# Two 64-wide attentions: reciprocal of the sums in four pieces between the maxima, product and more adds on GpSimd

## The reference, cut to what matters

```
# first layer, cross attention ("c"): 8 heads, queries from x (1024 a batch), keys and values from ctx (154 a batch)
sim = jnp.einsum('bihd,bjhd->bhij', q, k) * D ** -0.5
attn = jax.nn.softmax(sim, axis=-1)
out = jnp.einsum('bhij,bjhd->bihd', attn, v).reshape(B, Nq, H * D)

# first layer, feed-forward part ("m"): routed, 4 of 16 heads chosen for each batch, 1024 queries and 1024 keys
score = jax.nn.softmax(jnp.einsum('bhqd,bhkd->bhqk', Qs, Ks) * scale, axis=-1)
O = jnp.einsum('bhqk,bhkd->bhqd', score, Vs)
```

## Time and profile before

| | |
|---|---|
| median of 3 runs | 3031.12 us (3030.83 to 3033.93) |
| the profiled execution's own time | 3020.05 us |
| its span | 3018.5 us |
| busy of the span: TensorE / VectorE / ScalarE / GpSimd | 70% / 57% / 32% / 30% |
| mean granted TensorE clock over the span | 0.817 of 2.4 GHz |
| c: first maxima matmul to last product | 592.8 to 770.4 us |
| m: first exp to last product | 933.6 to 1133.9 us |

### The profile page before, as it was taken

One profiled execution on the slowest core, in us unless ns is written; L12 is line 12 of the kernel. 1 busy time (PEld: TensorE's weight loads), 2 busy tenths in 40 slices (PEclk: granted clock), 3 DMA queues, 4 the chain that ended last, 5 costly groups with the idle time before them and its releaser, 6 DMA issues. The chain is left out here.

```text
span 3018.5 us, 37236 instructions
## 1 busy us (share of the span) xinstructions
PE 2120.8 (70%) x13401; PEld 1081.7 (36%) x13405; DVE 1727.6 (57%) x3122; ACT 976.5 (32%) x1721; POOL 893.1 (30%) x1051
## 2 busy tenths in 40 slices
PE   3478888778557996299999981454485595529992
PEld 2224344322432224123333241232142253427992
DVE  2656664566537874277777515897774704436442
ACT  0246665133102331157777710111020020134330
POOL 0222221211022340457555311232263201052224
PEclk8779999878778997689999965555797797559996
DMA  4321110000010000501110032000110000053113
GB/s 133 157 59 37 43 43 7 18 1 0 10 25 1 1 1 16 198 12 32 33 32 25 9 99 66 1 2 3 42 56 28 14 30 4 24 183 126 50 50 94
DMA packets 86525, 133.20 MB, mean 44 GB/s; under 512 B 18309, under 2 KB 58257, under 8 KB 85329
## 3 DMA queue, kind: packets, MB, share of 16 engines
q1 hardware_dynamic: 76673, 118.70, 12.3%
q0 software_dynamic: 3664, 9.32, 1.0%
q10 hardware_dynamic: 6016, 2.89, 0.4%
HBM read 84.94 MB, written 45.68 MB: 43 GB/s over the span
## 5 line engine op out<-in xcount | busy, mean ns | idle before, releaser
L769 DVE TENSOR_REDUCE a_mneg<-a_SM 128x1 f32<-128x1024 f32 (+7 forms) x512 | 489.7, 986 | 232.4 <-PE a_SM L631 122.3
L752 ACT ACTIVATE a_P<-a_ST 128x512 f32<-128x512 f32 (+2 forms) x896 | 474.0, 556 | 243.1 <-PE a_ST L662 234.9
L631 PE MATMUL a_SM<-a_K,a_Q 96*128 96x512 bf16 (+2 forms) x896 | 271.8, 375 | 119.7 <-POOL a_V L583 109.0
L662 PE MATMUL a_ST<-a_Q,a_K 98*128 98x512 bf16 (+2 forms) x896 | 302.7, 368 | 17.3 <-ACT a_P L752 12.7
L680 PE MATMUL a_OP<-a_P,a_V 128*32 128x512 f32 (+3 forms) x1792 | 226.6, 567 | 5.2 <-ACT a_OT L732 3.5
L662 PEld LDWEIGHTS a_ST<-a_Q,a_K 98*128 98x128 bf16 x896 | 82.4, 103 | 242.6 <-ACT a_P L752 214.6
L631 PEld LDWEIGHTS a_SM<-a_K,a_Q 96*128 96x128 bf16 x896 | 85.7, 100 | 199.7 <-POOL a_V L583 109.7
L599 POOL TENSOR_SCALAR_AFFINE_SELECT a_P<-a_P 128x128 f32<-128x128 f32 (+1 forms) x256 | 77.1, 305 | 254.9 <-ACT a_P L752 252.9
L2775 DVE TENSOR_TENSOR experts_hl<-work 128x512 bf16<-128x512 f32 x92 | 83.8, 969 | 88.8 <-POOL work L2625 88.8
L2625 POOL CAST work<-work 128x512 bf16<-128x512 f32 x92 | 73.5, 838 | 198.9 <-PE experts_py L2709 183.7
L161 PE MATMUL n_turned<-ident,work 128*128 128x128 f32 x192 | 34.6, 365 | 133.5 <-DVE work L204 133.5
(11 more groups left out here) (504 smaller groups left out, 4475.2 us busy)
## 6 DMA issues: line engine op xcount, KB each, us to landing
work<-L_ffn_W SPq DMA_DIRECT2D x16, 1024.0 KB, 6.2
a_Q<-q_stacks SPq DMA_DIRECT2D x32, 384.0 KB, 3.8
a_K<-k_stacks SPq DMA_DIRECT2D x32, 384.0 KB, 4.7
conv_tab<-dft_tables SPq DMA_DIRECT2D x8, 1024.0 KB, 4.8
bias_hankel<-bias_rows SPq DMA_DIRECT2D x16, 448.0 KB, 3.4
k_stacks<-a_qkv_k_hi SPq DMA_DIRECT2D x12, 512.0 KB
q_stacks<-a_qkv_q_hi SPq DMA_DIRECT2D x12, 512.0 KB
expert_rows<-zeros SPq DMA_DIRECT2D x1, 5888.0 KB, 24.4
```

The costliest lines, as they stand in the source:

```text
L631: last = pe.matmul(SM[:, c % 2, k0:k0 + kn], Qs[0:KR, g % slots, u, qt * P:(qt + 1) * P], Ks[0:KR, g % slots, u, k0:k0 + kn], start=True, ...
L662: last = pe.matmul(out[:, c0:N], Ks[0:KX, g % slots, u, k * P:(k + 1) * P], Qs[0:KX, g % slots, u, qh * N + c0:(qh + 1) * N], start=True, ...
L752: act.activation(Pr[:, s % 2, u, j, c0:N], ST[:, (4 * s + x) % 2, c0:N], ACT.Exp, scale=scale).then_inc(exp_done, 1)
L769: dve.tensor_reduce(mneg[:, g % 2, u, qt:qt + 1], SM[:, c % 2, 0:width(qt)], AX.X, ALU.max, negate=True).then_inc(mx_read, 1)
```

## The change

The reciprocal of a unit's sums is made as four instructions of 128 columns each, `inverse(n, lo, hi)`, at hand-picked places of VectorE's loop; `den_read` now counts four a unit. The first number of a key of `pieces_at` is the step k, the second says whether the place is before (0) or after (1) the second maxima call; the value is how many units back, and the pieces. The product moves from VectorE to GpSimd, ahead of its add in a later step (`product_at`: step, units back). In m (`shared` True) each engine keeps its add, in c GpSimd makes both.

```
     if per > 2:
-        lead, rows_at, sums_at = 3, 6, 2
+        lead, rows_at, sums_at, shared = 3, 6, 2, True
+        pieces_at, product_at = {(2, 0): (1, 0, 1), (3, 0): (1, 1, 2), (4, 0): (1, 2, 3), (5, 0): (1, 3, 4)}, (6, 1)
     else:
-        lead, rows_at, sums_at = cpu + cpu // per, 0, 1
+        lead, rows_at, sums_at, shared = cpu + cpu // per, 0, 1, False
+        pieces_at, product_at = {(1, 0): (1, 0, 1), (1, 1): (1, 1, 3), (0, 0): (2, 3, 4)}, (1, 2)
...
             @block.gpsimd
             def _(pool):
+                def product(n):
+                    b, p, qh = units[n]
+                    q0 = b * S + qh * N
+                    pool.wait_ge(den_read, 4 * n + 4)
+                    pool.wait_ge(ot_done, n + 1)
+                    pool.tensor_tensor(YT[:, p, q0:q0 + N], OT[:, n % 2, :], R[:], ALU.mult).then_inc(y_done, 1)
+
                 pool.memset(MR[:], 0.0).then_inc(cleared, 1)
                 for s in range(ns):
+                    if product_event(s) is not None:
+                        product(product_event(s))
                     add(pool, s, 0, added0)
+                    if not shared:
+                        add(pool, s, 1, added1)
+                for n in range(product_event(ns - 1) + 1 if product_event(ns - 1) is not None else nu - 1, nu):
+                    product(n)
+                pool.wait_ge(y_done, nu)
...
                     if taken.sums:
-                        pe.wait_ge(den_read, taken.sums)
+                        pe.wait_ge(den_read, 4 * taken.sums)
...
-                def result(n):
-                    b, p, qh = units[n]
+                inverted = Shared()
+                inverted.n = 0
+
+                def inverse(n, lo, hi):
                     dve.wait_ge(den_ready, n + 1)
-                    if n:
+                    if n and lo == 0:
                         dve.wait_ge(y_done, n)
-                    dve.reciprocal(R[:], AUX[:]).then_inc(den_read, 1)
-                    dve.wait_ge(ot_done, n + 1)
-                    dve.wait_ge(den_read, n + 1)
-                    q0 = b * S + qh * N
-                    dve.tensor_tensor(YT[:, p, q0:q0 + N], OT[:, n % 2, :], R[:], ALU.mult).then_inc(y_done, 1)
+                    for x in range(lo, hi):
+                        dve.reciprocal(R[:, x * P:(x + 1) * P], AUX[:, x * P:(x + 1) * P]).then_inc(den_read, 1)
+                        inverted.n += 1
+
+                def inverse_event(s, slot):
+                    n, k = divmod(s, per)
+                    if (k, slot) in pieces_at:
+                        back, lo, hi = pieces_at[k, slot]
+                        if n >= back:
+                            inverse(n - back, lo, hi)
...
                     maxima(lo, cut)
-                    if s:
+                    if s and shared:
                         add(dve, s - 1, 1, added1)
-                    if sums_event(s) is not None:
-                        result(sums_event(s))
+                    inverse_event(s, 0)
                     maxima(cut, hi)
-                add(dve, ns - 1, 1, added1)
-                result(nu - 1)
-                dve.wait_ge(y_done, nu)
+                    inverse_event(s, 1)
+                if shared:
+                    add(dve, ns - 1, 1, added1)
+                while inverted.n < 4 * nu:
+                    inverse(inverted.n // 4, inverted.n % 4, 4)
```

More of the change, by code:

```diff
@@ L1088, in sums_event, with product_event @@
         return n - 1 if k == sums_at and n else None
+    def product_event(s):
+        n, k = divmod(s, per)
+        return n - product_at[1] if k == product_at[0] and n >= product_at[1] else None
     def adds(s):
```

## The result

The changed kernel took 2979.13 us in the median of 4 runs (2973.74 to 2979.87) against 3030.97 us (3030.08 to 3033.93): ratio 0.9826, 95% interval 0.9813 to 0.9839, 52 us faster. The prediction was 2987 us, 2970 to 3008, with 0.91 on faster. A second measurement gave 0.9818 (0.9794 to 0.9842).

What follows compares the result with a forecast made beforehand. TensorE's waits for VectorE's maxima reductions, and the half clock after them, were taken to bound c and m. Terms -30 (c), -14 (m), +0.9 and -0.5 (ends) gave about -44 us off 3031.12: 2987 us, range 2970 to 3008.

Steps and rivals of the forecast that it cites:

- What bounds the kernel: c and m: TensorE waits for VectorE's maxima reduction behind the reciprocal, 2.48 us in a c unit, then runs at half clock.
- Pieces: VectorE: a 128-column reciprocal takes 958 ns, 0.88 us start to start; four cost 3.5 us, 0.2 us more than before.
- Product and adds on GpSimd: c and m: 1.27 us each, upper bound 1.8; adds have 3.9 us slack in c; hold-up of VectorE put at nothing.
- c, hand schedule: Cross attention unit at full clock: 7.5 us, with two TensorE waits of 0.65 and 0.75 us instead of one of 2.48.
- The clock in c: Half-clock stretch adding about 1.2 us, reckoned in half of c's units: 8.1 us a unit, gain 30 us.
- A: The forecast case for c and m, chance 0.55: total from 2976 (no half clock in c) to 2994 us.
- B: Rival, chance 0.36: c's clock keeps falling in each unit, unit 8.7 to 9.3 us, total 2996 to 3003 us.
- m: Routed attention: unit from 25.67 to 23.3 us, 0.3 to 0.5 us stall in step 6; gain 14 us.
- Ends: Ends of the stages: m 0.9 us slower, c 0.5 us faster.
- C: Rival, chance 0.04: time hidden anyway or moved work returns as waits in c and m; within 6 us of before.
- D: Rival, chance 0.05: TensorE at half clock all through c, a unit 12.1 us; slower, 3038 us.

Runs made afterwards that it cites:

- e2: Changed kernel with the reciprocal whole again, one instruction of 512 columns at the first piece's place; product and adds stay on GpSimd: 2995.45 us, ratio 0.9907.
- e8: Changed kernel, c's pieces as halves around the second reduction, c's second add on VectorE behind the second reduction of the step without sums: 2973.82 us, ratio 0.9828.
- e3: Changed kernel with one thing undone: in c the second head's add is VectorE's again, before the last piece: 2995.42 us, ratio 0.9897.
- e9: As e8, with the product on VectorE too, in c behind the late add, in m in step 6: 2963.23 us, ratio 0.9806.

## Why the prediction was right, point by point

- **What bounds the kernel.** Right: TensorE waited for reductions behind the reciprocal, and in c paid again at the half clock. e2 shows both prices apart, 8.11 and 9.7 us. For m the prediction took one pair of units, 25.01 and 26.66 us, as wait and slow stretch; the unit of 25.01 us had the same wait, and three of the five kept the clock.
- **Pieces.** Estimated 958 ns and 0.88 us from start to start; two of them take 1.76 us, and single ones 0.94 to 0.96.
- **Product and adds on GpSimd.** Estimated 1.27 us each; the products take 1.27 in the median, and in the 12 units of c no one waited for them but VectorE's cast. It takes 822 ns in the median where it was 186, and 185 again in e8, where the product comes earlier than the cast. The prediction allowed a hold-up of these small instructions of up to 1.27 us and put its cost at nothing; it was 0.64 us, and nothing waited for it.

```profile
L1278 DVE CAST c_MR<-c_neg x16: 185/822/827, 605.2 to 714.2; 128x8 bf16<-128x8 f32 x16
```

- **c, hand schedule.** 7.4 to 7.5 us at the full clock; measured 7.38. The two waits were placed right and sized 0.65 and 0.75, measured 0.37 and 0.64 of idle time. The schedule counts four f32 passes as 0.86 us from start to start where the rows have them busy for 1.02, which is part of the difference; the rest stays open.
- **The clock in c.** This is the term that was mis-sized. "I reckon with such a stretch in half of the units: 8.1 us" failed: there was none, and the gain was 38.6 us, not 30. It was a guess between two levels, and no row that the prediction shows has waits this short, so that A came and not B was not worked out: in that it was luck. Its price of a slow stretch, 1.2 us, was low too: in e2 such a unit took 1.5 to 1.65 us more. Rival B, that two short waits do as well as one long one, was wrong here, but nearly right for one add more: e3's waits of 0.37 and 1.24 us bring B's unit of 9.25 us. The Trainium skill ("TensorE: Matmul & The Clock Gate", A second HAM failure mode) says that frequent small idles between groups of matmuls make the clock swing. This was seen in c with 0.37 and 1.24 us or with 1.67 us a unit, and not with 0.37 and 0.64 us or with 0.84 us.
- **m.** 23.3 us a unit and 14 us predicted, 23.08 and, with the sixth unit (22.68 to 19.66), 16.0 measured. The stall in step 6, estimated at 0.3 to 0.5 us, is not there: TensorE is busy 115.38 of 115.38 us in these five units. The 0.17 us above the hand sum of 22.9 is TensorE's own work, 23.09 us a unit before the change as well.
- **Ends.** c's tail, from the first reciprocal after the maxima to the last product, became 2.0 us shorter (23.17 to 21.14), not 0.5; m's stage as a whole lost 15.4, so its end cost about 0.6 us, predicted 0.9.
- **Rivals C and D.** No sign of either: the moved work is hidden, and c is not at the half clock.

The sum was -44 with c at 8.1 us; with 7.38 in its place it is -53, and the medians moved by 52 and 56. With every term as measured it is -38.6 - 16.0 - 2.0 + 0.6 = -56 us, the difference of the two stages in the profiles. The recorded range does not follow from its own terms: A's lower end, 2976, less 2 us is 2974, and B's upper end, 3003, plus 8 us is 3011, not 2970 and 3008; the measured time is inside either.

## What to carry to other kernels

When an engine serves a single-buffered hand-over, look at what stands between two services in its order, not at its busy share: a long instruction that nobody is waiting for can be cut up or moved behind the service, and can stay on the same engine (e9). A wait that also brings TensorE's clock down can cost about three times its length (0.6 us more in e3 cost 1.9), so read the clock unit by unit, and try what the next shortening does: in c the step from 1.24 to 0.64 us (e3 to the changed kernel) brought 1.87 of the 3.2 us a unit gained, in m waits of 0.94 to 1.07 us a unit cost no clock.

## What the runs showed of the hardware

A reciprocal of 128x128 f32 from PSUM takes 0.94 to 0.96 us and four in a row 3.39, against 3.36 for one of 512 columns, so cutting it is almost free. A cast of eight columns on VectorE took 0.82 us beside GpSimd's product and 0.19 without it, while the pieces and reductions from PSUM kept their lengths.

In c, waits of 0.37 and 0.64 us, or one of 0.69 or 0.84, per 7.2 to 7.5 us left the clock at 1.00 in all units; 0.37 with 1.24 brought it to 1.2 GHz in eleven of twelve units, one of 1.67 in eight of twelve. In m, one wait of 0.94 or 1.07 us in 24.2 us left it at 1.00, and one of 1.92 in 25 us brought it down in two units of five. In c the longest wait and the sum of the waits rise together from run to run (at most 0.84 and 1.01 us where the clock stood in all units, at least 1.24 and 1.61 where it fell in most), so these runs don't tell which of the two counts, and nothing was measured between them.
